# Fused gated linear attention and ternary FFN: two rounding remainders exchanged between VectorE and GpSimd, and the transposes of x2 put ahead of the last product's first passes on TensorE

## The reference, cut to what matters

```python
# x: (4, 512, 128); 16 heads of 8 channels
x = layernorm(x + attn(x))
x = layernorm(x + ffn(x))

# attn: q, k, v = x@Wq, x@Wk, x@Wv;  gate = exp(log_sigmoid(x@Wgk1@Wgk2 + b) / 16)
#   state = state * gate + v k^T   (a scan over the 512 tokens),   out_t = state q_t
#   out = layernorm(out) * gamma + beta;  out = out * silu(x@Wg);  return out @ Wout
# ffn: h = silu(x@w1.T * s1) * (x@w2.T * s2)      128 -> 512
#      h = gelu(h@h1.T * s);  h = gelu(h@h2.T * s)     512 -> 512, twice
#      return h@w3.T * s3                          512 -> 128
```

## Time and profile before

| what | value |
|---|---|
| median of 3 runs | 178.25 us (177.07 to 178.44) |
| the profiled execution's own time | 178.06 us |
| its span, first to last instruction | 176.3 us |
| TensorE busy | 160.1 us, 91% |
| VectorE busy | 137.3 us, 78% |
| ScalarE busy | 116.8 us, 66% |
| GpSimd busy | 111.8 us, 63% |

### The profile page before, as it was taken

The page is one execution under the profiler, slowest core; times in us unless marked ns, Lnnn a source line. Parts: engine busy times, 40 slices in busy tenths (PEclk is TensorE's granted clock), DMA queues, the critical chain, the costliest instruction groups (busy, mean ns, idle before and its releaser), DMA issues.

```text
span 176.3 us, 2661 instructions
## 1 busy us (share of the span) xinstructions
PE 160.1 (91%) x778; PEld 119.9 (68%) x778; DVE 137.3 (78%) x278; ACT 116.8 (66%) x211; POOL 111.8 (63%) x109
## 2 busy tenths in 40 slices
PE   0899999999888999998999999899999999999980
PEld 0766667868656676876868678587666875887870
DVE  0689889967798997599999975999996695854062
ACT  5444789993236836187787468677978578995721
POOL 8707987969907779983477998919684250803132
PEclk9999999999999999999999999999999999999999
DMA  4999910244100000000000000000002000040102
GB/s 111 329 396 414 393 48 0 51 129 121 60 4 0 2 0 0 4 0 2 0 0 0 0 0 0 0 0 0 0 0 65 0 0 0 2 114 23 55 8 63
DMA packets 7455, 10.55 MB, mean 60 GB/s; under 512 B 753, under 2 KB 5394, under 8 KB 6930
## 3 DMA queue, kind: packets, MB, share of 16 engines
q1 hardware_dynamic: 6866, 7.50, 13.8%
q0 software_dynamic: 576, 2.88, 4.2%
HBM read 8.55 MB, written 1.84 MB: 59 GB/s over the span
## 4 chain that ended last, share of the span: by engine, by line
POOL 18%; PE 14%; DVE 13%; issue 12%; ACT 6%; DVEq 1%; POOLq 0%; ACTq 0%
POOL u_tok L345 7%; DVE state L1152 5%; POOL f_lo L406 4%; PE ffn L667 3%; POOL o_acc L360 3%; PE ffn L658 2%; DVE y L1164 2%; PE ffn L636 2%; PE ffn L641 1%; ACT last_f L1108 1%; PE att L580 1%; POOL o_rstd L368 1%; POOL r_rstd L368 1%; PE ffn L682 1%; ACT f_hi L938 1%
## 5 line engine op out<-in xcount | busy, mean ns | idle before, releaser
L1152 DVE TENSOR_TENSOR_SCAN state<-gate,att 128x512 f32<-128x512 f32 x32 | 38.4, 1209 | 0.8 <-PE att L580 0.8
L406 POOL TENSOR_TENSOR f_lo<-full,f_hi 128x512 fp32r<-128x512 f32 x18 | 23.0, 1293 | 20.2 <-DVE full L1238 14.9
L946 ACT ACTIVATE f_hi<-ffn,vec_cols 128x512 fp32r<-128x512 f32 x24 | 16.5, 686 | 19.8 <-PE ffn L667 19.6
L658 PE MATMUL ffn<-f_hi,h_hi 128*128 128x512 f32 x96 | 28.2, 407 | 0.2
L667 PE MATMUL ffn<-f_lo,h_hi 128*128 128x512 f32 x96 | 26.1, 398 | 0.0
L360 POOL TENSOR_TENSOR o_acc<-o_acc,y 128x512 f32<-128x512 f32 x16 | 20.6, 1290 | 8.6 <-DVE y L1164 8.5
L345 POOL TENSOR_TENSOR u_tok<-kv_tok 128x1024 f32<-128x1024 f32 x12 | 25.5, 2136 | 0.1
L580 PE MATMUL att<-ident,u_tok 128*128 128x128 f32 x128 | 20.2, 285 | 2.1 <-POOL u_tok L345 1.3
L658 PEld LDWEIGHTS ffn<-f_hi,h_hi 128*128 128x128 f32 x96 | 17.6, 188 | 5.8 <-ACT f_hi L946 1.5
L580 PEld LDWEIGHTS att<-ident,u_tok 128*128 128x128 f32 x128 | 15.7, 146 | 7.3 <-DVE state L1152 2.9
L667 PEld LDWEIGHTS ffn<-f_lo,h_hi 128*128 128x128 f32 x96 | 17.8, 188 | 3.7
(11 more groups left out here) (188 smaller groups left out, 354.5 us busy)
## 6 DMA issues: line engine op xcount, KB each, us to landing
h_raw<-in_hT SPq DMA_DIRECT2D x2, 1024.0 KB, 12.0
h_hi<-in_hT POOLq DMA_DIRECT2D x2, 1024.0 KB, 11.6
x_tok<-in_x SPq DMA_DIRECT2D x4, 256.0 KB, 4.7
out<-out_tok SPq DMA_DIRECT2D x3, 256.0 KB, 2.3
w_raw<-in_w12T SPq DMA_DIRECT2D x1, 512.0 KB, 4.3
w_hi<-in_w12T POOLq DMA_DIRECT2D x1, 512.0 KB, 8.6
q_swap<-q_hi SPq DMA_DIRECT2D x3, 128.0 KB, 2.5
q_swap<-q_lo SPq DMA_DIRECT2D x3, 128.0 KB, 2.4
```

What stands on the lines that cost most here:

```text
L406: nc.gpsimd.tensor_tensor(lo[:, o], full_block(layer, o), hi[:, o].bitcast(F32), ALU.subtract).then_inc(pool_rested, 1)
L658: nc.tensor.matmul(bank[:], h_hi[:, layer - 1, c, tile(o)], src_hi[:, c], start=(c == 0), stop=False)
L946: nc.scalar.activation(hidden[layer][0][:, o], bank[:], ACT.Gelu, scale=scales[:, 1 + layer, o:o + 1]).then_inc(gelu_hi_ready, 1)
L1152: nc.vector.tensor_tensor_scan(state[:, k % 3], gate[:, b], A[2 + k % 2][:], 0.0, ALU.mult, ALU.add).then_inc(scanned, 1)
```

## The change

The remainder of block (1, 1) goes from GpSimd to VectorE, where it stands in `attention_end` behind that of (1, 2), ahead of `apply_gate`. The remainder of block (2, 3) goes from VectorE's `make_x2` to GpSimd, behind the last outer product of `attention_end`. With them the exact value of (1, 1) is now put in its PSUM bank, and that of (2, 3) in slot 0 of `full`; ScalarE gets two waits that guard this slot. On TensorE `transpose_x2(a)` goes ahead of `ffn_out_hi`.

```diff
-        ON_POOL = [(0, 0), (0, 1), (0, 2), (1, 0), (1, 1)]
-        ON_DVE = [(0, 3), (1, 2), (1, 3), (2, 1), (2, 0), (2, 2), (2, 3)]
+        ON_POOL = [(0, 0), (0, 1), (0, 2), (1, 0), (2, 3)]
+        ON_DVE = [(0, 3), (1, 2), (1, 1), (1, 3), (2, 1), (2, 0), (2, 2)]
...
                 outer_products(a + 1, last_tiles)
+                if a >= 1:
+                    rest(a - 1, 2, 3)
...
                 rest(b, 1, 0)
-                rest(b, 1, 1)
...
                 ffn_hidden_rest(f, 2, 3)
+                transpose_x2(a)
                 ffn_out_hi(f, with_lo)
-                transpose_x2(a)
...
             def ffn_silu(b, o):
                 act.wait_ge(a_ready, OB * b + o + 1)
+                if o == 0 and b >= 1:
+                    act.wait_ge(*rested(b - 1, 2, 3))
...
+                if (layer, o) == (2, 3):
+                    act.wait_ge(*rested(b, 1, 0))
...
                 rest(f, 1, 2)
+                rest(f, 1, 1)
                 apply_gate(a)
...
                 rest(f, 2, 2)
-                rest(f, 2, 3)
                 rest_of_x2(a)
```

## The result

The changed kernel takes 178.51 us (median, 177.31 to 179.62), the kernel before, run on the same chip in turn with it, 177.83 us (177.07 to 178.61). The ratio is 1.0039, with a 95% interval of 1.0021 to 1.0057: slower by 0.7 us (0.37 to 1.0). That is within 1%, as forecast, and 178.4 lies close. But the change in time is twice the +0.34 us of the sum. That the number comes so close is luck: it stood on the profiled execution of 178.06 us, and the median of before is 177.83 in the longer measurement.

A forecast was written before the change was run, and what follows sets the result against it. It took VectorE's full scan stretches and the chain over all engines between them to bound the kernel; 0.26 + 0.08 + 0 = +0.34 us on 178.06 gave 178.4 us, range 177.2 to 179.6.

The forecast's parts named there:

- the sum: Total of the terms at the ends of three steps: 0.26 (A) + 0.08 (B) + 0 (C, the last) = +0.34 us.
- VectorE's remainders, cost nothing: Ahead of the gate, 0.64 us more work fits a 1.1 us wait; ahead of `x_lo`, 0.64 less becomes a wait.
- GpSimd: `o_var` 0.18 us earlier in B, nothing in A and C: Behind GpSimd's outer products, `o_var` wins 0.18 us in the second step only; the rest of 1.28 becomes a wait.
- The moved transposes: At a step's end on TensorE, four passes now follow the transposes of x2: 0.26 us later in A, 0.08 in B.
- L675 from 80.31: On TensorE in the first step, the four passes start 0.03 us behind the fourth transpose's start at 80.28.
- The scan of k=1 decides: At the start of VectorE's full stretch, the second scan has no slack and starts 0.26 us later in A.
- Step C, 0: In the last step, with no next row, `yT` waits for its table load anyway: 0 us, about 0.1 to spare.
- The clock stayed: Rival on TensorE: standing drops its clock to 1.2 GHz, 7.4 us over three steps, 185.4 us; chance 0.03.
- The gain of several us: Rival at the step's end: GpSimd's and VectorE's queues bind, A and B win 3.8 us, 174.2 us; chance 0.05.
- only B's gain: Rival at the step's end: A gives 0 and B -0.18 us, 177.9 us; chance 0.17.
- wholly exposed: Rival on TensorE: each of three steps pays 1.02 us for the four passes, 181.1 us; chance 0.10.

The follow-up runs named there:

- e8: Only the remainder of block (1, 1) moved to VectorE, against the kernel before; ratio 1.0010 to the kernel before.
- e1: The change without its moved transposes, so only the two remainders exchanged, against the kernel before; ratio 1.0003 to the kernel before.
- e3: On e1, the transposes of x2 put behind two of the last product's four first passes and ahead of the other two; ratio 0.9992 to the kernel before.
- e5: The change with TensorE's hardware loop over its first two steps written out, so waits are against constants; ratio 1.0017 to the kernel before.
- e4: The change with the transposes of k=1 put ahead of the last product's second pass set; ratio 1.0039 to the kernel before.
- e6: e4 with the VectorE scan's wait for its transposes put behind its other waits; ratio 1.0046 to the kernel before.
- e9: On e1, GpSimd's outer products of tiles 2 and 3 made in halves, both scans' transposes and layer 0 moved up on TensorE; ratio 0.9955 to the kernel before.
- e2: Only the transposes of x2 moved ahead of the four passes, both remainders left, against the kernel before; ratio 1.0055 to the kernel before.

## Why the prediction was right, and where its sum was off

- **VectorE's remainders, cost nothing: right.** The wait ahead of the gate fell from 1.1 to 0.51 us (0.46 expected), and the 0.64 us less ahead of `x_lo` became a wait of 0.45 us for `x_hi`.
- **GpSimd: `o_var` 0.18 us earlier in B, nothing in A and C: right.** In B it starts at 105.84, 4.13 us ahead of the last pass of (2, 3), where before it was 3.95; e8 shows it alone. The remainder of (2, 3) was taken to be in time for L682. With the order of the change it is; in e1, with the order of before, it is 0.07 us late.
- **The moved transposes: right in mechanism, too small in size.** `x_hi` did not come earlier (it starts 0.36 us behind the fourth transpose, before 0.37), and the four passes came behind the transposes. The term was +0.26 in A and +0.08 in B, and it measured +0.50 and +0.31. The step that failed is "L675 from 80.31": I took 0.03 us from the fourth transpose to the first pass, from groups whose instructions were ready long before. Behind an instruction that is itself waiting, the register instructions for the next wait's values are run only once it goes (e3, e5 and step C, with fewer or none of them in this place, have 0.09 to 0.10 us), and the distance was 0.27 us (L676 at 80.14, the fourth transpose at 79.87). That is 0.24 too little in each step, as much as is missing. The smaller terms were off too, and nearly cancel: in A the fourth transpose comes 2.73 us behind the last pass of (2, 3) and not 2.69, the four passes take 1.04 and not 1.02, and from the transposes of k=0 to L683 it is 0.35 and not 0.41. e5, without the register instructions, comes to the predicted steps in its profile, with a distance of 0.10 us, which is still not 0.03.
- **The scan of k=1 decides: wrong as far as it was the only one.** The prediction let the first scan start in time, with 0.05 us to spare. It comes late too: its transposes end at 81.18 + 0.60 = 81.78 and it starts at 82.08, 0.30 us behind, where the prediction has 0.07 for the second scan. So the new wait of 0.53 us stands ahead of the first scan, not of some 0.3 ahead of the second. And e4 and e6 show a third thing behind the two scans, the layer-0 passes that feed the FFN products. All three hang on TensorE's list behind L676, and the first scan, the transposes of k=1 and layer 0 are each 0.50 us late in A against the last pass of (2, 3), so the sum did not need to know which one decided.
- **Step C, 0: right**, 0.02 us. `yT` starts 0.02 us behind the end of its table load as before, and TensorE's fifth pass of the next layer comes 5.70 us behind the last pass of (2, 3), before 5.68.
- **The clock stayed.** View of stretches, after:

```profile
66.00:83.50 17.50, 16.75 (x79) 12.45 (x78) 13.84 (x38) 10.61 (x15) 13.63 (x11) 1.00 0.01 1
82.00:102.00 20.00, 19.42 (x96) 14.55 (x95) 19.67 (x25) 13.94 (x28) 13.09 (x11) 1.00 0.00 0
```

  The granted clock is 1.00, which is 2.4 GHz, in the stretch with the standing TensorE too: it has only four transposes from the end of the last pass (78.23) to 80.14. The Trainium skill ("TensorE: Matmul & The Clock Gate", "Part 4: PE-mode transpose") says that transposes do not count as activity for the clock as matmuls do; this trace neither bears that out nor refutes it. The second row is for comparison with the earlier trace rows: VectorE is busy 19.67 of 20.00 us, so what is lost ahead of it stays lost.
- **The rivals.** The gain of several us did not come; e8 bears out the case that only B's gain is there if the transposes stay. The four passes were not wholly exposed: 1.02 us in each step would be +2 us in A and B, and +0.81 was measured. From the fourth transpose to the transposes of k=0 it was 0.79 us before (80.28 to 81.07), its own time and the 0.46 for `u_tok`, and the passes run in that time too; in the change it is 1.31 (79.87 to 81.18).

## What to carry to other kernels

Putting a blocked instruction ahead of ready work in an in-order list exposes all of that work, except for what fits into a wait further down the same list: find that wait first, here 0.46 us against four passes of 1.02 us. When a queue is relieved, ask what its engine waits for next before counting a gain; the relief is worth something only if the freed room is used, as in e9, which won 0.8 us on top of an exchange that alone won nothing (how much of it e9's order would win without the exchange was not tried). In a hardware loop, count the instructions that compute a wait's value as work behind the instruction that waits.

## What the runs showed of the hardware that I had not expected

- TensorE's register instructions behind a waiting transpose: 0.27 us from the load of the fourth transpose to that of the next group in the loop (0.26 and 0.35 in the two steps of e2), 0.07 us with the loop written out. On VectorE, in the loop, the scan of k=0 starts 0.30 us behind the modelled end of its transposes when the wait that ends last is the first of its waits, and 0.15 us when it is the last (e6).
- Four transposes in 1.9 us, and nothing else on TensorE, left the granted clock at 1.00.
- The same remainder of 128 x 512 takes 1.29 us on GpSimd and 0.68 us on VectorE, so the exchange moves more time on GpSimd's side than on VectorE's.
